# Last stage of a mixture-of-experts block: shared down weights split by GpSimd in the stage before, 28 of 96 row gathers issued there, 44 homes for gathered rows

## The reference

```python
scores = sigmoid(x @ gate_w)                       # 32 experts
... 6 experts chosen per token, weights normalised
g = ragged_dot(xs, w_gate, group_sizes)            # rows sorted by expert
u = ragged_dot(xs, w_up, group_sizes)
d = ragged_dot(silu(g) * u, w_down, group_sizes)
expert_out = sum(d[unsorted] * weights, axis=1)    # 6 rows per token
shared = silu(x @ sw_gate) * (x @ sw_up) @ sw_down # 704 hidden channels
x = x1 + expert_out + shared
```

## Time and profile before

| | us |
|---|---|
| three timed runs | 2541.97, 2542.68, 2547.25 |
| median | 2542.68 |
| the profiled execution, device time | 2540.25 |
| its span (first to last instruction) | 2538.6 |
| PE busy in the span | 2261.1 (89%) |
| POOL busy | 1428.7 (56%) |
| DVE busy | 1254.2 (49%) |
| ACT busy | 1171.8 (46%) |

### The profile page before, as it was taken

The page is one execution under the profiler, slowest core; times in us unless marked ns, Lnnn a source line. Parts: engine busy times, 40 slices in busy tenths (PEclk is TensorE's granted clock), DMA queues, the critical chain, the costliest instruction groups (busy, mean ns, idle before and its releaser), DMA issues. The chain is left out here.

```text
span 2538.6 us, 42000 instructions
## 1 busy us (share of the span) xinstructions
PE 2261.1 (89%) x12059; PEld 1934.9 (76%) x12060; DVE 1254.2 (49%) x2120; ACT 1171.8 (46%) x2505; POOL 1428.7 (56%) x976
## 2 busy tenths in 40 slices
PE   1579999999999989898987989999999799999665
PEld 1458888888878877677766779999988699989554
DVE  6737777778755666867542322222222122222365
ACT  3347777777777767776621123333332133333210
POOL 7647777777754466665623036250669956420376
PEclk6789999999999999999988989999999899999887
DMA  4244345434355455553357045352547655522466
GB/s 122 70 121 126 112 129 161 140 112 125 109 166 175 132 167 170 184 178 125 100 199 278 1 137 179 109 160 99 177 158 224 202 165 181 191 96 79 127 199 185
DMA packets 285670, 372.37 MB, mean 147 GB/s; under 512 B 20212, under 2 KB 187192, under 8 KB 280824
## 3 DMA queue, kind: packets, MB, share of 16 engines
q1 hardware_dynamic: 229112, 251.41, 31.8%
q10 hardware_dynamic: 41088, 69.22, 8.3%
q0 software_dynamic: 15360, 50.34, 6.1%
HBM read 257.66 MB, written 113.25 MB: 146 GB/s over the span
## 5 line engine op out<-in xcount | busy, mean ns | idle before, releaser
L1918 POOL TENSOR_SCALAR we_high<-we_raw 128x1408 fp32r<-128x1408 f32 (+1 forms) x95 | 133.7, 1408 | 416.0 <-PE up_e L649 316.8
L1920 POOL TENSOR_TENSOR we_low<-we_raw,we_high 128x1408 fp32r<-128x1408 f32 (+1 forms) x95 | 314.4, 3309 | 7.9
L2034 DVE TENSOR_TENSOR hT_low<-hT_ps,hT_high 128x256 fp32r<-128x256 f32 x127 | 53.9, 424 | 391.3 <-ACT hT_high L1997 391.3
L2047 DVE TENSOR_TENSOR hidden_e<-silu_e,up_e 128x352 f32<-128x352 f32 x127 | 66.2, 521 | 284.2 <-ACT silu_e L2008 284.2
L2008 ACT ACTIVATE silu_e<-gate_e 128x352 f32<-128x352 f32 x127 | 59.0, 465 | 317.5 <-PE up_e L649 317.5
L649 PE MATMUL gate_e<-we_high,xT_high 128*128 x508 | 177.7, 350 | 19.7 <-POOL we_low L1920 19.4
L2013 ACT ACTIVATE rows_out<-down_e 128x512 f32<-128x512 f32 x127 | 75.9, 597 | 215.4 <-PE down_e L649 215.4
L649 PE MATMUL gate_e<-we_high,xT_low 128*128 x508 | 166.0, 327 | 0.0
L649 PE MATMUL gate_e<-we_low,xT_high 128*128 x508 | 165.7, 326 | 0.0
L649 PE MATMUL up_e<-we_high,xT_high 128*128 x508 | 165.2, 325 | 0.0
L649 PE MATMUL up_e<-we_low,xT_high 128*128 x508 | 163.9, 323 | 0.0
(11 more groups left out here) (341 smaller groups left out, 7312.0 us busy)
## 6 DMA issues: line engine op xcount, KB each, us to landing
rows_early<-slots_in ACTq DMA_DIRECT2D x129, 256.0 KB, 2.7
slots_out<-rows_out ACTq DMA_DIRECT2D x127, 256.0 KB, 2.1
we_raw<-L_ffn_w_gate SPq DMA_DIRECT2D x32, 704.0 KB, 4.5
we_raw<-L_ffn_w_up SPq DMA_DIRECT2D x32, 704.0 KB, 5.0
q_T<-q_out SPq DMA_DIRECT2D x64, 256.0 KB, 2.3
q_raw<-q_T SPq DMA_DIRECT2D x16, 1024.0 KB, 6.8
w_ring<-L_attn_Wk SPq DMA_DIRECT2D x64, 256.0 KB
w_ring<-L_attn_Wv SPq DMA_DIRECT2D x64, 256.0 KB
```

What stands on the lines that cost most here:

```text
L1918: nc.gpsimd.tensor_scalar(wh[:, p, at:to], raw[:, at:to], 1.0, 1.0, ALU.mult, ALU.mult).then_inc(w_hi, 1)
L1920: nc.gpsimd.tensor_tensor(wl[:, p, at:to], raw[:, at:to], wh[:, p, at:to].bitcast(F32), ALU.subtract).then_inc(w_split, 1)
L2047: nc.vector.tensor_tensor(hb[:], sg[:], psu[:], ALU.mult).then_inc(h_done, 1)
```

## The change

Five parts.

1. **Split moved.** In `experts`, SyncE no longer loads x1 but `sd_raw`, behind the last expert's weights. GpSimd, behind its last expert split, makes `sd_high` and, once expert 30 is through, `sd_low`, which now lies in the first buffer of `we_low`.
2. **28 early gathers.** GpSimd then waits until all blocks that hold rows have been stored (a count read from `blocks[31]`), and issues the first 28 of the 96 gathers, tiles 0 to 3 and four of tile 4, while TensorE goes on with the spare blocks. They land in 28 places of 512 columns that are free by then: `we_high` buffer 0, `we_raw`, `x_batch`, `sd_raw`, the rest of `we_low` buffer 0.
3. **44 homes.** In `combine` the buffers 1 of `we_high` and `we_low` give 16 more. Gather number i lands in home i mod 44 and waits for VectorE only from number 44 on. Indices are read from `yslot` directly; `slot_tile` and the copies go.
4. **x1 tiles from DRAM.** SyncE loads each tile of x1 (128 partitions, four pieces of 512 bytes in each) straight into `x_tile`; ScalarE's copies go. There are four PSUM banks instead of two, the six weights are read from `wts` without a copy, the 16 tiles are written out without loops, and `h_low` of tile n+2 stands behind the sums of tile n.
5. **Zero blocks.** Because a gather is now issued before the spare blocks are written, the 31 blocks that can be spare are filled with zeros earlier: GpSimd clears a tile in `first_gates`, SyncE stores it to DRAM, and at the start of the last eight attention iterations ScalarE issues one DMA from DRAM to DRAM of four blocks (three the last time), 31 blocks of 256 KB in all.

```diff
@@ first_gates
+            pool.wait_ge(ident_steps, 2)
+            nc.gpsimd.memset(zero[:], 0.0).then_inc(ident_steps, 1)
...
@@ attention, ScalarE
+            def zero_blocks(j):
+                first = NREAL + SPARE * j
+                n = min(SPARE, NBLK - first)
+                act.dma_start(dr["ys"][first * P:(first + n) * P, :].rearrange("(n p) c -> p n c", p=P),
+                              dr["zeros"].unsqueeze(1).broadcast_to([P, n, C])).then_inc(keep["spare_out"], 16)
...
+                if it >= NFIRST:
+                    zero_blocks(it - NFIRST)
...
@@ experts
+EARLY_ROWS = 28
+def row_homes(keep):
+    flat = lambda t: (t if t.dtype == F32 else t.bitcast(F32))[:, 0:t.shape[1] // C * C].rearrange("p (k c) -> p k c", c=C)
+    homes = (flat(keep["we_high"][:, 0, :]), flat(keep["we_raw"][:]), keep["x1"][:], keep["sd_raw"][:],
+             flat(keep["we_low"][:, 0, len(SCH) * C:]), flat(keep["we_high"][:, 1, :]), flat(keep["we_low"][:, 1, :]))
+    return [home[:, k, :] for home in homes for k in range(home.shape[1])]
...
-            for b in range(B):
-                sp.dma_start(xT[:, b, :, :], dr["x1"][b].rearrange("p (k s) -> p k s", k=KC)).then_inc(x1_in, 16)
+            sp.dma_start(sd_raw[:, 0:full, :], sw_down[0:full * P, :].rearrange("(k p) c -> p k c", p=P)).then_inc(sd_in, 16)
+            sp.dma_start(sd_raw[0:tail, full, :], sw_down[full * P:, :]).then_inc(sd_in, 16)
...
@@ experts, GpSimd, behind the last split
+            pool.wait_ge(sd_in, 32)
+            for rows, ks in parts:
+                last = nc.gpsimd.tensor_scalar(sd_h[rows, ks, :], sd_raw[rows, ks, :], 1.0, 1.0, ALU.mult, ALU.mult)
...
+            used = pool.value_load(blocks[0:1, E - 2:E - 1], min_val=1, max_val=NBLK)
+            pool.wait_ge(d_mm, used + CREDIT)
...
+            for rows, ks in parts:
+                last = nc.gpsimd.tensor_tensor(sd_l[rows, ks, :], sd_raw[rows, ks, :], sd_h[rows, ks, :].bitcast(F32), ALU.subtract)
...
+            real = pool.value_load(blocks[0:1, E - 1:E], min_val=NREAL, max_val=NBLK)
+            pool.wait_ge(y_ev, real + (CREDIT + 2))
...
+            for i in range(EARLY_ROWS):
+                t, k = divmod(i, TOPK)
+                pool.indirect_dma_start(homes[i], None, dr["ys"],
+                                        bass.IndirectOffsetOnAxis(ap=yslot[:, t, k:k + 1], axis=0)).then_inc(early_in, 16)
+            pool.wait_ge(early_in, 16 * EARLY_ROWS)
@@ combine, SyncE
+            def load(n):
+                if n >= 2:
+                    sp.wait_ge(o_mm, n - 1)
+                b, t = divmod(n, TC)
+                sp.dma_start(xc[:, n % 2, :, :], dr["x1"][b].rearrange("p (k s) -> p k s", k=KC)[:, :, at(t)]).then_inc(x_in[n % 2], 16)
...
@@ combine, GpSimd
+            for i in range(EARLY_ROWS, NT * TOPK):
+                n, k = divmod(i, TOPK)
+                if i == EARLY_ROWS or not k:
+                    if sum(gathered[n % 2:n:2]):
+                        pool.wait_ge(y_in[n % 2], 16 * sum(gathered[n % 2:n:2]))
+                if i >= len(homes) and (i == len(homes) or not (i - len(homes)) % TOPK):
+                    pool.wait_ge(o_done, (i - len(homes)) // TOPK + 1)
+                pool.indirect_dma_start(row_of(i), None, dr["ys"],
+                                        bass.IndirectOffsetOnAxis(ap=yslot[:, n, k:k + 1], axis=0)).then_inc(y_in[n % 2], 16)
...
@@ combine, VectorE
+            low(0)
+            low(1)
+            for n in range(NT):
+                p = n % 2
+                dve.wait_ge(o_mm, n + 1)
...
+                    nc.vector.scalar_tensor_tensor(out=(ob if last else acc)[:, p, :], in0=row_of(TOPK * n + k), scalar=wts[:, n, k:k + 1],
+                                                   in1=acc[:, p, :] if k else pso[n % 4][:], op0=ALU.mult,
+                                                   op1=ALU.add).then_inc(o_done if last else acc_done, 1)
+                if n + 2 < NT:
+                    low(n + 2)
```

More of the change, by code:

```diff
@@ L140, in _ @@
                 load_wq(j)
+            sp.wait_ge(ident_steps, 3)
+            sp.dma_start(dr["zeros"], zero[:]).then_inc(keep["spare_out"], 16)
             def store_xT(n):
@@ L163, in _ @@
             sp.wait_ge(xt_out, 16 * KC)
+            sp.wait_ge(keep["spare_out"], 16)
         @block.gpsimd
@@ L1363, in _ @@
                         averaged(n)
+            act.wait_ge(keep["spare_out"], 16 * (NIT - NFIRST + 1))
         @block.vector
@@ L2049, in _, with combine @@
             pipeline(dve, NBLK, 2, 2, step)
-def combine(nc, keep, dr, sw_down, out):
-    xT, ident, hsh, wts, slot = (keep[k] for k in ("xT", "ident", "hsh", "wts", "yslot"))
+def combine(nc, keep, dr, out):
+    ident, hsh, wts, yslot = (keep[k] for k in ("ident", "hsh", "wts", "yslot"))
     NS = len(SCH)
+    tail = SCH[-1][1]
     with ExitStack() as ctx:
@@ L2072, in combine @@
-        pool_steps, act_steps = keep["pool_steps"], keep["act_steps"]
-        block = ctx.enter_context(nc.Block())
-        tail = SCH[-1][1]
-        def loop(eng, step):
-            with eng.Fori(0, B) as b:
-                for t in range(TC):
-                    step(TC * b + t, t % 2, (TC // 2) * b + t // 2, b, t)
+        xc, acc = sb("x1_tile", [P, 2, KC, P]), sb("acc", [P, 2, C])
+        ob = keep["early"][:, 0:2, :]
+        homes = row_homes(keep)
+        row_of = lambda i: homes[i % len(homes)]
@@ L2093, in _ @@
-            loop(sp, step)
-            for p in range(2):
-                sp.wait_ge(o_out[p], 16 * NT // 2 + 16)
+            def load(n):
[3 more added lines that the diff above has]
+                sp.dma_start(xc[:, n % 2, :, :], dr["x1"][b].rearrange("p (k s) -> p k s", k=KC)[:, :, at(t)]).then_inc(x_in[n % 2], 16)
+            load(0)
+            load(1)
+            for n in range(NT):
+                if n + 2 < NT:
+                    load(n + 2)
+                b, t = divmod(n, TC)
+                sp.wait_ge(o_done, n + 1)
+                sp.dma_start(out[b, at(t), :], ob[:, n % 2, :]).then_inc(o_out[n % 2], 16)
@@ L2204, in build @@
         ys=dram("slots_out", [NBLK * P, C]),
+        zeros=dram("zero_block", [P, C]),
     )
```

166 lines of the change are left out of this document (68 added, 98 removed).

## The result

The changed kernel took 2555.73 us (median of six runs, 2545.15 to 2565.76) beside 2542.47 for the kernel before (2541.80 to 2547.43): ratio 1.005, interval 1.0031 to 1.007. It is slower by 13 us; forecast were 2489.8 us and a chance of 0.03 for slower. In later groups of runs, each taken together on one chip, the same two kernels gave another answer: 2468.92 against 2524.15, ratio 0.978 (0.9758 to 0.9802). The device stands in one of two conditions: the kernel before takes 2520 to 2525 us in one (called A here) and 2540 to 2545 in the other (B). One chip showed both. Each trace also tells its condition, ahead of the experts' stage: GpSimd issues 24 indirect DMAs in a row there, which scatter the last batch's rows, and from the first of them to the first expert split are 109.8 us in all thirteen traces of A and 127.0 to 129.4 us in all seven of B.

A forecast was written before the change was run, and what follows sets the result against it. GpSimd's gather issue was taken to bound the last stage. GpSimd's path 2483.7 plus 1 (DMA) plus 1 (zeros) gave span 2485.7, 53 less; from the median, 2489.8 us, range 2479 to 2508.

The forecast's parts named there:

- The step that failed: In `experts`: the early split and 28 gathers hide with 50 us of cover, cost 0, bounds -1 and +3.
- The prediction's own sign: Check on `experts`: it ends where it did, within 3 us, counted from attention's end.
- the early gathers do not hide: Rival in `experts`: early gathers fail to hide because the experts' transfers suffer; some 2510 us, chance 2%.
- The last stage: `combine`: 68 gathers from 2373.5, last tile's first sum at 2476.4, span end 2483.7 before 1 us for DMA.
- TensorE at 5.5 us a tile: `combine`: TensorE needs 5.5 us per tile at the full granted clock, VectorE 5.7.
- The pitch: `combine`: time per GpSimd gather beside VectorE's sums, taken as 1.5 us; bounds 1.39 and 1.57.
- GpSimd's path: `combine`: eight gathers at 1.26 us, 60 at 1.5, then data and sums; span end 2483.7, bounds 2477 and 2488.
- Zeros: Attention iterations: eight bursts of zero blocks cost 1 us, bounds 0 and 42.
- the 10 to 42 of the rival: Rival in attention: zero bursts lie in the path, 10 to 42 us back, 2500 to 2532; chance 9%.
- Starvation of gathers beside VectorE: Rival in `combine`: each gather waits for one whole sum, 2.0 us each; 2518 in the runs, chance 11%.
- the lock held over several sums: Rival in `combine`: SBUF contention blocks each gather over several sums, 3.27 + 0.30 us each; chance 3%.
- Slower than before: Rival in `combine`: gathers blocked over several sums, 3.57 us each; span 2608, 2612 in the runs; chance 3%.

The follow-up runs named there:

- e15: Changed kernel with at most two early gathers under way, condition B: 2520.17 us against 2545.08 for the kernel before, ratio 0.9899.
- e17: Changed kernel with its 28 early gathers replaced by plain DMAs from SyncE, condition B: median 2525.63 us, ratio 0.9938 against the kernel before.
- e18: Changed kernel unaltered, run again in condition B: ratio 1.0069 against the kernel before.
- e1: Kernel before with only the zero blocks (part five) added, condition A: 2526.44 us against 2520.64, ratio 1.0016.
- e6: Changed kernel unaltered, run again in condition A: 2468.92 us against 2524.15 for the kernel before, ratio 0.978.
- the flood: Changed kernel with 56 copies of 256 KB from DRAM to DRAM beside the early gathers, condition B: ratio 1.0054 against the kernel before.

## Why the prediction was wrong, point by point

**The step that failed** is "so all of this hides [...] I cost the experts at 0 (bounds -1 and +3)". It cost 31.6 us. The reasoning looked at buffers, at the DMA engines' share (0.23) and at GpSimd's idle time, and all of these were right: the gathers took their 1.26 us, and share and bytes turned out not to matter. It left out that a dense run of GpSimd's gathers could itself hold up TensorE. The prediction's own sign, that `experts` ends where it did within 3 us, was missed tenfold. The case "the early gathers do not hide" had 2%, some 2510 us, and for the wrong reason (the experts' transfers). e15, e17 and e18 show the cause as far as it is shown: the tail is 143 with gathers two by two or with plain DMAs, 174 with the dense ones. What passes between GpSimd and the others stays open.

**The last stage** was to be 110 us from its first gather and was 145. This is the second term that was mis-sized. The forecast took TensorE at 5.5 us a tile from the earlier trace rows, a tile without pauses. It starves here too: 8.0 us of pauses within tiles, and in five tiles signals that come 2.2 to 19.6 us late, 39.6 us together. The stage is 39 us longer than in A (106.1); the two sums needn't agree, since such waits overlap others. That the cause is the experts' is argued from the same signs; no run in condition B took its gathers away. Against it stands `combine` of the kernel before, in B as well: 96 gathers, every pause of TensorE stands before a tile's first product and none within a tile, and ScalarE starts 0.20 us behind each tile. There a copy parts every six gathers, and four tiles are looped over instead of sixteen written out. Which of the differences counts wasn't tested.

**The sign in the profile of before** was there, and I passed over it, 100 us ahead of the experts' stage (whose first transposes stand at 1463.4 us; it doesn't start at 1360). The 24 scatters of the last batch stand there at a pitch of 1.28 us beside a TensorE that has products in plenty. The busy times of 35 us from the first scatter, of the kernel before (B), then of e1 (A), whose code is the same there:

```profile
1334.96:1369.96 35.00, 22.13 (x84) 16.11 (x82) 5.13 (x20) 1.80 (x3) 23.47 (x24) 0.80 0.89 337
```

```profile
1343.84:1378.84 35.00, 35.00 (x157) 28.88 (x156) 11.34 (x29) 4.54 (x7) 23.98 (x24) 1.00 1.03 390
```

And TensorE and ScalarE of the kernel before in this stretch:

```profile
1357.87 0.58 PE L649 MATMUL up_ps<-x_low,sw_high 128*128 128x512 f32 x1 [2.32 <-issue]
1364.19 0.59 PE L649 MATMUL up_ps<-x_low,sw_high 128*128 128x512 f32 x1 [2.21 <-issue]
...
1369.23 0.60 ACT L1740 ACTIVATE silu_g<-gate_ps 128x512 f32<-128x512 f32 x1 [23.52 <-remote]
```

It is the stall of the early gathers in all its marks: steps between neighbouring products, one long wait of ScalarE for TensorE, TensorE at 22.13 us of work where A has 35.00. It makes the 18 to 20 us by which B is longer from these scatters to the first split, and so nearly all of the difference between the conditions (about 20 us by the medians of the kernel before). The prediction looked at the DMA traffic of this very stretch and took its 398 GB/s for stores of zero rows; 64.3% of the DMA engines' time in it went to the scatters' queue.

The mark "issue" alone isn't the sign. These are the waits of TensorE's weight loads in `combine` of the kernel before in B, 2400 to 2530 us, and of e1 in A, 2392 to 2521 us:

```profile
PEld out_ps L649 <- issue: 33.1, 24, 6.7
```

```profile
PEld out_ps L658 <- issue: 25.8, 20, 7.3
```

They are of one size in both conditions and belong to no stall: these pauses stand between tiles, where TensorE waits for VectorE.

**The pitch** of 1.5 was too high where nothing starves: 1.41 in e6, close to the lower bound of 1.39. In condition B it is 1.60, but 15.1 of its 107.1 us are the two waits for VectorE (8.38 and 6.68); without them it is 1.37.

**GpSimd's path in condition A**: forecast 110 us from the first gather to the end, 106.1 measured: 4.4 less up to the last gather's start (94.2 us and not 98.6), by the pitch, and 0.2 more behind it (11.9 us and not 11.7). First sum on VectorE 8.8 us behind the first gather, forecast 10.9.

**Zeros**: 1 us taken, 4 measured (e1). Right in kind, four times too small; at no point near the 10 to 42 of the rival.

**Starvation of gathers beside VectorE**, and the lock held over several sums, did not come: in neither condition did a gather of the changed kernel's last stage take more than 1.65 us, and with 0.30 of issue only one reached 1.95; these rivals wanted 2.0 and 3.6 for each. Slower than before did come true, by a mechanism that no rival had.

**The range** 2479 to 2508 held neither condition's time (2468.92 in A, 2555.73 in B). Part of that is the starting point: all rows were of condition B, with the stall beside the scatters in them. As a ratio, the forecast's 0.979 is what A gave.

## What to carry to other kernels

Look for pauses of an engine within a run of instructions that nothing in the code holds up, and for starts that come long after the result they wait for has ended, and see what another engine does at that moment: before a change puts more of it there, price it in. Work moved beside a busy engine uses more than the buffers and bandwidth it names: in condition B a dense run of indirect DMAs held up TensorE, and through it the others, so space them (two under way cost nothing in A, where there was time to hide them, and saved 31 us in B). And when a kernel and its experiments stop agreeing, run the unaltered kernel again beside them before believing a cure.

## What the hardware showed that I had not expected

- In condition B, GpSimd's indirect DMAs at 1.26 us each hold up TensorE, with steps of up to 2.2 us between neighbouring products, and its signals: two engines that wait for the same one start together up to 19.6 us late. TensorE, VectorE and ScalarE all went to 0.00 busy in 10 us. At 2.12 us each the gathers don't do it (29.57 of 30). Scatters at 1.28 us do it as gathers do (22.13 us of TensorE's work in 35, against 35.00 in A).
- A quarter of the bytes at the same pitch starves as much (4.11 of 20 us at a DMA share of 0.23); as many bytes in plain DMAs don't (19.78 of 20 at 0.82).
- The same chip showed the same kernel at 2524.15 and at 2545.08, and the changed one's tail at 142.4 and (with the flood) 178.7 us. Up to the last batch's scatters the conditions don't differ: the first of them starts at 1340.46 us in e6 (A) and at 1339.05 in e18 (B), the first expert split at 1450.25 and 1466.37. What the two conditions are stays open; nothing in a trace of A foretells B.
